# Reciprocal of the softmax denominators on VectorE, evacuation of q and k on ScalarE, in a four-layer attention block

## The reference, cut to what matters

```python
def _attn(x, W_qkv, b_qkv, W_ao, b_ao):
    b, s, d = x.shape
    qkv = jnp.einsum('bsd,od->bso', x, W_qkv) + b_qkv
    qkv = qkv.reshape(b, s, 3, H, DH)
    q, k, v = ...
    scores = jnp.einsum('bhqd,bhkd->bhqk', q, k) * SCALE
    wts = jax.nn.softmax(scores, axis=-1)
    o = jnp.einsum('bhqk,bhkd->bhqd', wts, v)
    o = jnp.moveaxis(o, 1, 2).reshape(b, s, d)
    return jnp.einsum('bsd,od->bso', o, W_ao) + b_ao
...
for l in range(L):
    m = _mamba(x, ...)
    x = _ln(x + m, g1[l], be1[l])
    a = _attn(x, W_qkv[l], b_qkv[l], W_ao[l], b_ao[l])
    x = _ln(x + a, g2[l], be2[l])
    h = gelu(x @ W_f1[l].T + b_f1[l]); x = x + h @ W_f2[l].T + b_f2[l]
```

## Time and profile before

| | value |
|---|---|
| median of 3 runs | 2846.8 us |
| profiled execution | 2852.53 us |
| span of its records | 2850.8 us |
| granted TensorE clock, mean | 0.900 |
| attention of layer 0, first to last step | about 150 to 430 us |
| a steady step in it | 15.1 to 17.5 us |
| PE, DVE, ACT, POOL busy | 82%, 59%, 58%, 25% |

### The profile page before, as it was taken

One profiled execution on the slowest core, in us unless ns is written; L12 is line 12 of the kernel. 1 busy time (PEld: TensorE's weight loads), 2 busy tenths in 40 slices (PEclk: granted clock), 3 DMA queues, 4 the chain that ended last, 5 costly groups with the idle time before them and its releaser, 6 DMA issues.

```text
span 2850.8 us, 54378 instructions
## 1 busy us (share of the span) xinstructions
PE 2327.4 (82%) x16356; PEld 1476.7 (52%) x16356; DVE 1686.2 (59%) x2866; ACT 1645.8 (58%) x2539; POOL 700.1 (25%) x976
## 2 busy tenths in 40 slices
PE   6978889977888987888997888969756699996885
PEld 4544445644444644444564444546654477764575
DVE  4567753657773556774465777356323678865642
ACT  6447775636776645777554777655432156665452
POOL 0123210012221012231002232117563100002754
PEclk8969989978999996999997999989877799998997
DMA  2033310023330013331003332041321233324133
GB/s 108 20 102 92 113 47 6 8 76 93 110 92 7 9 32 99 104 102 36 14 0 91 100 102 79 7 82 50 113 72 36 74 94 98 97 59 85 51 115 124
DMA packets 137819, 199.42 MB, mean 70 GB/s; under 512 B 15681, under 2 KB 91969, under 8 KB 137409
## 3 DMA queue, kind: packets, MB, share of 16 engines
q1 hardware_dynamic: 128448, 178.45, 21.9%
q0 software_dynamic: 9216, 19.02, 1.8%
HBM read 98.04 MB, written 96.76 MB: 68 GB/s over the span
## 4 chain that ended last, share of the span: by engine, by line
PE 50%; issue 12%; DVE 11%; POOL 10%; DMA 9%; ACT 5%; SPq 2%; DVEq 1%; POOLq 1%; ACTq 0%
PE ps L1047 7%; PE ps L1072 6%; POOL back_scratch L2566 5%; POOL slot_scratch L2561 5%; DVE hmx L2095 4%; PE ps L853 4%; DMA hqk<-hmt 3%; PE ps L816 2%; PE ps L780 2%; DMA hqk<-hqk_scratch 2%; PE ps L786 2%; PE ps L892 2%; DMA hqk_scratch<-hqks 2%; PE ps L731 2%; PE ps L928 2%
## 5 line engine op out<-in xcount | busy, mean ns | idle before, releaser
L2095 DVE TENSOR_REDUCE hmx<-ps 128x2 f32<-128x512 f32 x768 | 506.8, 688 | 222.8 <-PE ps L1047 218.5
L1635 ACT ACTIVATE hpt<-ps 128x1024 f32<-128x1024 f32 x512 | 519.9, 1020 | 61.9 <-PE ps L1059 61.0
L1047 PE MATMUL ps<-hqk 24*128 24x256 f32 x2048 | 307.3, 359 | 153.3 <-DVE hmx L2095 99.4
L1047 PEld LDWEIGHTS ps<-hqk 24*128 24x128 f32 x2048 | 197.3, 208 | 366.6 <-DVE hmx L2095 255.1
L1072 PE MATMUL ps<-hpt,hvx 128*32 128x256 f32 x4096 | 304.1, 419 | 15.9 <-ACT hpt L1635 15.4
L1059 PE MATMUL ps<-hqk 26*128 26x256 f32 x2048 | 273.8, 349 | 2.4 <-ACT hpt L1635 1.6
L1656 ACT ACTIVATE hrow<-ps 128x512 f32<-128x512 f32 x256 | 151.9, 593 | 203.0 <-PE ps L1047 203.0
L2103 DVE TENSOR_REDUCE hmx<-hrow 128x2 f32<-128x512 f32 x256 | 176.0, 687 | 45.2 <-ACT hrow L1656 35.9
L1059 PEld LDWEIGHTS ps<-hqk 26*128 26x128 f32 x2048 | 163.4, 198 | 23.9 <-ACT hpt L1635 18.4
L2566 POOL DMA_INDIRECT back_scratch<-ys,xslot x160 | 153.2, 958 | 86.6 <-issue 47.9
L2003 DVE TENSOR_REDUCE mxs<-ps 128x2 f32<-128x512 f32 x256 | 164.0, 680 | 14.8 <-PE ps L892 13.6
(11 more groups left out here) (299 smaller groups left out, 5243.5 us busy)
## 6 DMA issues: line engine op xcount, KB each, us to landing
hqk_scratch<-hqks SPq DMA_DIRECT2D x64, 768.0 KB, 3.2
hqk<-hqk_scratch SPq DMA_DIRECT2D x256, 192.0 KB
qk_scratch<-qks SPq DMA_DIRECT2D x16, 768.0 KB, 3.3
slot_scratch<-filler SPq DMA_DIRECT2D x10, 1040.0 KB, 15.9
xslot<-slot_scratch SPq DMA_DIRECT2D x20, 520.0 KB
yback<-back_scratch SPq DMA_DIRECT2D x32, 256.0 KB, 4.5
k<-qk_scratch SPq DMA_DIRECT2D x16, 384.0 KB
qv<-qk_scratch SPq DMA_DIRECT2D x64, 96.0 KB
```

The costliest lines, as they stand in the source:

```text
L1047: return mm(ps[:, o % 2, qt * SEQ:(qt + 1) * SEQ], hqk[r][32 * g:32 * g + 24, j, 0, qt * P:(qt + 1) * P], hqk[r][32 * g:32 * g + 24, j, 1, ...
L1635: A(hpt[:, j, g:g + 2, :, :], ps[:, 2 + g:4 + g, :], ACT.Exp, scale=QSCALE).then_inc(hd_exp, 1)
L2095: V.tensor_reduce(hmx[:, r, :, 4 * g + j], ps[:, o % 2, :].rearrange("p (t k) -> p t k", t=2), AX.X, ALU.max).then_inc(hd_max[o % 2], 1)
```

## The change

Three things. The logarithm and exponential of `reciprocal(b)` leave ScalarE; VectorE does one `RECIPROCAL` of the 128x512 denominators from PSUM bank 7 to `hrec` instead, after part 4's maxima. The evacuation of q and k in the steps leaves VectorE and goes to ScalarE, after part 3's exponential (ScalarE's function for it exists already, for the first three sequences of a layer). And the semaphore `hd_ln`, which said that bank 7's denominators had been read, is replaced by `hd_rec`, which says that the reciprocal is done.

```diff
@@ TensorE, step
                                 if first:
                                     pe.wait_ge(hd_q, nth(hd_q, B + 3, 1))
                                 else:
-                                    pe.wait_ge(hd_ln, nth(hd_ln, B - 1))
+                                    pe.wait_ge(hd_rec, nth(hd_rec, B - 1))
                                 maxima(b + 1)
...
                             if n1:
                                 pe.wait_ge(hd_mt, nth(hd_mt, B + 1))
                             else:
-                                pe.wait_ge(hd_ln, nth(hd_ln, B - 1))
+                                pe.wait_ge(hd_rec, nth(hd_rec, B - 1))
                             out(b - 1)
...
                 def last_out():
-                    pe.wait_ge(hd_ln, nth(hd_ln, l * BATCH + 15))
+                    pe.wait_ge(hd_rec, nth(hd_rec, l * BATCH + 15))
                     out(15)
@@ ScalarE
-                def reciprocal(b):
-                    B = l * BATCH + b
-                    act.wait_ge(hd_sel, nth(hd_sel, B))
-                    act.wait_ge(hd_on, nth(hd_on, B - 1))
-                    A(hrec[:].rearrange("p x n -> p (x n)"), ps[:, 7, :], ACT.Ln).then_inc(hd_ln, 1)
-                    act.wait_ge(hd_ln, nth(hd_ln, B))
-                    A(hrec[:], hrec[:], ACT.Exp, scale=-1.0).then_inc(hd_rec, 1)
...
-                        if p == 4 and not first:
-                            reciprocal(b - 1)
+                        if p == 3 and n3:
+                            evac_qk(b + 3)
...
-                norm(l * 2 + 2, hooks={(0, 0): head_attention(l, "end")[0]})
+                norm(l * 2 + 2, hooks={"apart": None})
@@ VectorE
-                def evac_qk(b):
-
-                    B = l * BATCH + b
-                    dve.wait_ge(hd_qk, nth(hd_qk, B))
-                    dve.wait_ge(hd_parts, nth(hd_parts, B - 1))
-                    for a, bias in enumerate(("bq", "bk")):
-                        V.tensor_scalar(hqk32[:, a, :], ps[:, 7, a * SEQ:(a + 1) * SEQ], T(bias), None, ALU.add)\
-                         .then_inc(hd_q, 1)
...
+                def reciprocal(b):
+                    B = l * BATCH + b
+                    dve.wait_ge(hd_sel, nth(hd_sel, B))
+                    dve.wait_ge(hd_on, nth(hd_on, B - 1))
+                    V.reciprocal(hrec[:].rearrange("p x n -> p (x n)"), ps[:, 7, :]).then_inc(hd_rec, 1)
...
-                        if p == 3 and n3:
-                            evac_qk(b + 3)
+                        if p == 4 and not first:
+                            reciprocal(b - 1)
...
-                    return [lambda: add_out(15)]
+                    return [lambda: reciprocal(15), lambda: add_out(15)]
...
-                     hooks={(0, 2): end[0],
+                     hooks={(0, 0): end[0], (0, 2): end[1],
```

More of the change, by code:

```diff
@@ L415, in build_program @@
         hd_sel = counter("hd_sel")
-        hd_ln = counter("hd_ln")
         hd_rec = counter("hd_rec")
@@ L1676, in head_attention @@
                     return [lambda: evac_qk(0), first_v, lambda: evac_qk(1)]
-                if part == "end":
-                    return [lambda: reciprocal(15)]
                 evac_qk(2)
```

## The result

The changed kernel takes 3131.8 us (median of four runs, 3119.9 to 3134.5), 1.0995 times the kernel before (95% interval 1.0967 to 1.1023; before 2843.2 us, median of four). The forecast was 3041 us in a range of 2960 to 3140. The direction was right, and so was the loop between VectorE and TensorE as the place where the reciprocal costs; but the largest term of the growth, TensorE's clock, was hardly in the sum. Of the growth of about 290 us the forecast named two thirds. The profiled execution took 3119.9 us, with a span of 3118.1 us, 267 us over the span before.

What follows compares the result with a forecast made beforehand. Bound: the loop of VectorE and TensorE waiting for each other. Per layer 38.4 + 1.0 + 1.0 + 6.2 = 46.6 us, 186 for four, plus 8 for the clock: 194 on 2846.8, forecast 3041 us, range 2960 to 3140.

Steps and rivals of the forecast that it cites:

- The cheap: VectorE's reciprocal has mainly a fixed cost and takes 0.77 us: 12 us a layer, 2895 us in all; chance 7%.
- the proportional: All of the reciprocal's time grows with its elements, 8.1 us: 285 us more, 3326 us in all; chance 3%.
- the eight-cycle: Reciprocal at eight cycles an element, 4.4 us, 1.07 us more in about 15 places a layer: 3105 us; chance 12%.
- Steps (2): ScalarE, steady step: the evacuation of q and k waits behind part 3's exponential, ending at 329.2 instead of 327.90.
- (3): TensorE, steady step: denominators wait for ScalarE's evacuation, both in bank 7, and start at 329.35 instead of 328.03.
- Step (5): Given back: part 5's transposes no longer hold part 6's rows; maximum 4.1 us late, steady step 3.2 us longer.
- the loop term: Steady steps with an evacuation, 12 a layer, each 3.2 us longer: 38.4 us a layer.
- Step (9): TensorE's clock: gaps of about 2 us bring two more dips a layer, 8 us in all; bounds 0 and 38.
- 3139 us as a rival with 5%: TensorE's clock falls for its gaps in half of the steps, 4.1 us each: 98 us, 3139 in all; chance 5%.
- Step (8): Layer's end, step 15 and behind: reciprocal, then quotient, make `out(15)` start at 439.95 instead of 433.78, 6.2 us.
- step (7): Step 13: part 5's maximum later, 1.0 of 2.7 us lasting; step 14: reciprocal holds the transposes, 1.0 us.
- the three signs of being wrong: Reciprocal under 2 us, denominators not late, or steps longer for TensorE's clock: any would show the forecast wrong.

Runs made afterwards that it cites:

- experiments 1: Changed kernel with VectorE's reciprocal replaced by a copy of the same 128x512, same place and waits: 2886.8 us, 1.0148 of the kernel before.
- experiment 6: Changed kernel with the reciprocal over half of the columns (128x256) and a copy for the other half: 2905.7 us, 1.0206 of the kernel before.
- experiment 3: Changed kernel with two useless 128x512 matmuls on TensorE in the gap before the transposes: 2990.2 us, 1.0512 of the kernel before.
- experiment 10: experiment 3 with the layer's last reciprocal back on ScalarE as logarithm and exponential: 2956.4 us, 1.039 of the kernel before.
- experiment 2: Changed kernel with the evacuation of q and k back on VectorE, so only the reciprocal is moved: 3055.9 us, 1.0722 of the kernel before.
- experiment 7: Changed kernel with one useless matmul on TensorE before the transposes, where experiment 3 has two: 2997.5 us, 1.0527 of the kernel before.

## Why the prediction was right, and where it was short

**The bound.** VectorE and TensorE waiting for each other between maxima was the right reading. But the instruction did not go into the step whole: of its 3.36 us 2.1 did, at full clock, since the loop had some slack that the first part of it filled (experiments 1 and 6: 0.1 to 0.2 us a step for a copy of 0.69, 0.8 for 2.1). What came on top of that went in whole, with VectorE at 60% busy.

**The price of the reciprocal.** 3.35 us forecast, 3357 ns measured; experiment 6 gives the same 6.25 ns an element. The fixed part came out at 157 ns for the 153 taken. That the neighbour with 16 elements was the right one to take it from was a choice; the other two values that the prediction weighed give 2.0 and 4.4 us. The cheap, the proportional and the eight-cycle rivals are out. The last was read from the Trainium skill ("VectorE: DVE Perf Modes", walkthrough of the 8-slice pipeline); by these rows an element takes 6 cycles of its 0.96 GHz, whatever the repeat count of 8 counts.

**Steps (2) and (3) failed: the late denominators.** I had the evacuation on ScalarE end 1.3 us later, since I took the two exponentials in the earlier trace rows (2.04 us) for those of parts 2 and 3. They are those of parts 3 and 4: part 3's starts right behind that part's row copy, and the evacuation slots in between the two. The row of part 4's rows before is

```profile
326.62 0.38 PE L1047 MATMUL ps<-hqk 24*128 24x256 f32 x2
```

From there to the denominators it was 1.41 us (326.62 to 328.03); it is 1.50 us in the changed kernel (343.00 to 344.50). VectorE idled 0.93 us for them, not 2.1. So part 5's maximum is 2.9 us late by the same measure (6.02 us behind part 4's rows, for 3.13), not 4.1.

**Step (5), what is given back,** was about right: 0.9 us forecast (4.1 became 3.2), 0.8 measured (2.9 became 2.1 at full clock, 17.2 us in experiment 3 for 15.1). At full clock the loop term is 48 x 2.1 = 101 us; I had 154, because of the late denominators.

**Step (9) failed: the clock**, 8 us with a bound of 38, and 3139 us as a rival with 5%. (Its own product, 4 x 2 x 1.2, is 9.6 and not 8.) All 44 counted steps were touched by the low clock, not two more in a layer. From experiment 3's span of 2983.8 to 3118.1 it is 134 us, the largest term of all. My mistake was to price the fall by the earlier trace rows, where a mean of 0.90 costs 1.2 us. Here it came with nearly every step and at a place where the loop has no slack to hide it: 3.3 us, of which the output projection alone is 0.95 (2.08 against 1.13) and each round of rows and maxima a few tenths. The rival had a price nearer to that (4.1 us) and half the steps. I held against it that the gaps are only 2 us long with matmuls between them; that was the error. The Trainium skill's rule ("TensorE: Matmul & The Clock Gate", Part 1), a halved clock behind an idle stretch, agrees with this trace in kind: in the step shown the granted clock goes from 1.00 to 0.50 behind 2.10 us of idle.

**Step (8), the layer's end.** 6.2 us forecast with step 15; from sequence 14's add to 15's it is 22.5 us for 14.9, 7.6 more, and experiment 10 gives 27 us of span for the four layers. The chain was as written (reciprocal, quotient, projection). Of the 1.4 us above the forecast, 0.9 is the output projection at the low clock (2.04 us for 1.10).

**The sum.** Times of each profiled execution, added over the four layers, in us; experiment 3 stands for the changed kernel with the clock held up:

| | before | experiment 3 | changed |
|---|---|---|---|
| first 11 distances between adds | 689.3 | 758.1 | 885.4 |
| next 3 | 166.3 | 191.4 | 194.9 |
| last (layer's end) | 59.4 | 94.2 | 90.4 |
| all else | 1935.8 | 1940.2 | 1947.5 |

The clock in the steady steps is the 127 us from 758.1 to 885.4. The loop is the 69 us from 689.3 to 758.1, less than 44 x 2.1 = 92, because the kernel before loses some 25 us there itself, over 44 x 15.1, mostly to its own low clock. (The first step of each layer with a reciprocal is under "all else".) The layers' ends are 31 us, for 25 forecast. The three distances ahead of them are 29, for which the prediction's step (7) had 8, and how much of that is loop and how much clock no run separates.

**Luck.** At full clock the loop was forecast 53 us too long (154 for 101), and the clock some 120 us too short; the two errors partly cancel. The range held 3131.8 us by 8 us, and its upper end, 3140, was worked out from a reciprocal of 4.4 us and more dips, which is not what happened. Of the three signs of being wrong that the prediction names, two came true: the denominators were not late, and steps became longer for TensorE's clock.

## What to carry to other kernels

Where two engines wait for each other with no spare buffer, price an instruction by its place between their exchanges, and not by its engine's busy share: at 59% busy, VectorE hid 1.3 us of a 3.36 us instruction and no more. Then look at the gap it leaves on TensorE: here a gap of 2.1 us in each step cost more through the clock that followed (3.3 us) than the instruction cost in the loop (2.1). And the price of an operation that the trace had only small came out well as its small row less the fixed part of a neighbour of the same size.

## What the runs showed of the hardware

- VectorE's reciprocal in fp32 from PSUM: 1757 ns for 128x256, 3357 ns for 128x512. A copy of the same 128x512 took 691 ns; ScalarE's logarithm and exponential together 1227 ns.
- How many of 44 steady steps were touched by TensorE's low clock, by the idle stretch before the transposes: all at 2.10 us (changed kernel), 30 at 1.87 to 1.94 us (experiment 2), 8 at 1.05 us (experiment 7), 6 at 0.78 us (experiment 6), 1 at 0.19 us (experiment 3). So a longer gap made a fall more frequent. It does not decide alone: the step at 853.04 passed at full clock with 2.10 us, and experiment 6's six are all in layer 0, while its layers 1 to 3 have none with the same gap. The kernel before has no such gap and 12 falls, which stay unexplained. No run puts the filler elsewhere in the step, so whether this gap counts or TensorE's idle time in the step as a whole is open.
- Two useless matmuls in each step made a kernel 142 us faster, 4.5% of its time.
